# Four chained graph layers on one core: row sums divided out on GpSimd before the transposes, layer 0 multiplied by rows, query and key stacks copied without a spill

## What is computed

```python
# layer 0
agg = einsum('bij,bjf->bif', adj, x) / maximum(sum(adj, -1), 1e-6)
out = relu(concat([x, agg], 2) @ W.T)
# layer 1: e from x, alpha = adj * exp(leaky_relu(e)), T = alpha / (row sum + 1e-12)
out = relu(x @ Wk0 + (T @ x) @ Wk1 + (T @ T @ x) @ Wk2 + biases)
# layer 2: three times adj @ (x @ W) + b, the first two with relu
# layer 3: 8 heads of 32
scores = einsum('bhqd,bhkd->bhqk', q, k) * SCALE * (adj + adj)[:, None]
attn = softmax(scores, axis=-1)
ctx = einsum('bhqk,bhkd->bhqd', attn, v)
out = ctx @ Wo.T + bo
```

## Time and profile before

| | us |
|---|---|
| median of 3 runs (3450.55 to 3451.14) | 3451.12 |
| profiled execution, its own time | 3450.14 |
| its span | 3448.3 |
| PE busy | 3168.9 (92%) |
| DVE busy | 2149.7 (62%) |
| ACT busy | 1749.3 (51%) |
| POOL busy | 405.7 (12%) |

### The profile page before, as it was taken

How to read it: one execution, slowest core, us unless ns; L and a number is a source line. 1 busy time by engine, 2 the same in 40 slices (tenths; PEclk the granted TensorE clock), 3 DMA queues, 4 the chain that set the end, 5 groups by cost and what they waited for, 6 DMA issues and landing times.

```text
span 3448.3 us, 79514 instructions
## 1 busy us (share of the span) xinstructions
PE 3168.9 (92%) x27032; PEld 2727.9 (79%) x27032; DVE 2149.7 (62%) x3916; ACT 1749.3 (51%) x3025; POOL 405.7 (12%) x1613
## 2 busy tenths in 40 slices
PE   6999989999899998999989999899997999989998
PEld 5887779877798677986779877798776987779877
DVE  4636866268662685637856378553786537865387
ACT  3425844258442684426844268432674326743277
POOL 0101110011100111000110001100111001110011
PEclk9999999999999999999999999899998999989999
DMA  5113132131320313303133031330313303123120
GB/s 198 50 54 85 48 124 64 41 84 48 124 79 29 84 45 124 97 14 88 42 121 99 13 87 47 116 99 13 87 48 114 99 25 78 57 103 98 36 49 17
DMA packets 147694, 252.43 MB, mean 73 GB/s; under 512 B 11047, under 2 KB 112172, under 8 KB 147244
## 3 DMA queue, kind: packets, MB, share of 16 engines
q1 hardware_dynamic: 147244, 246.73, 22.2%
HBM read 146.03 MB, written 100.66 MB: 72 GB/s over the span
## 4 chain that ended last, share of the span: by engine, by line
PE 45%; issue 40%; DMA 5%; DVE 4%; POOL 3%; ACT 2%; DVEq 1%; SPq 0%; POOLq 0%; ACTq 0%
PE ps L655 10%; PE ps L645 7%; PE ps L454 7%; PE ps L456 7%; PE ps L455 7%; PE ps L668 5%; DMA qk_spill<-u_lo 3%; DMA k_stack<-qk_spill 2%; PE ps L683 1%; POOL shift L427 1%; POOL vare L420 1%; DVE r L1307 1%; DVE stats L1104 1%; DVE xr L1338 1%; POOL rstd L423 0%
## 5 line engine op out<-in xcount | busy, mean ns | idle before, releaser
L1307 DVE CUSTOM_DVE_ANT_0 r<-ps,adjn 128x1024 f32<-128x1024 f32 x512 | 621.9, 1217 | 31.5 <-PE ps L655 19.5
L1014 ACT ACTIVATE r<-r,nmax 128x1024 f32<-128x1024 f32 x512 | 585.7, 1144 | 80.7 <-POOL nmax L446 80.7
L655 PEld LDWEIGHTS ps<-ident,r 128*128 128x128 f32 x4096 | 471.0, 142 | 118.6 <-DVE pt L1316 75.6
L655 PE MATMUL ps<-ident,r 128*128 128x128 f32 x4096 | 551.3, 278 | 3.5 <-DVE pt L1316 3.5
L454 PE MATMUL ps<-u_hi,t_hi 128*128 128x256 f32 x1536 | 447.0, 291 | 4.1 <-DVE u_lo L1067 4.1
L455 PE MATMUL ps<-u_lo,t_hi 128*128 128x256 f32 x1536 | 439.0, 286 | 0.0
L456 PE MATMUL ps<-u_hi,t_lo 128*128 128x256 f32 x1536 | 438.8, 286 | 0.0
L1316 DVE COPY pt<-ps 128x512 f32<-128x512 f32 x512 | 353.1, 690 | 136.3 <-PE ps L655 136.2
L645 PE MATMUL ps<-k_stack,q_stack 96*128 96x512 f32 x1024 | 377.9, 452 | 54.5 <-DVE mmax L1307 32.4
L816 ACT ACTIVATE pt<-ps 128x512 f32<-128x512 f32 x512 | 304.9, 595 | 180.1 <-PE ps L655 175.4
L454 PE MATMUL ps<-w_hi,xt_hi 128*128 128x256 f32 x1024 | 302.0, 295 | 32.3 <-DVE xt_lo L1074 27.1
(11 more groups left out here) (172 smaller groups left out, 5556.1 us busy)
## 6 DMA issues: line engine op xcount, KB each, us to landing
adjn<-in_adj SPq DMA_DIRECT2D x64, 512.0 KB, 3.4
t_spill<-t_hi SPq DMA_DIRECT2D x64, 512.0 KB, 2.6
t_spill<-t_lo SPq DMA_DIRECT2D x64, 512.0 KB, 3.7
t_hi<-t_spill SPq DMA_DIRECT2D x32, 1024.0 KB, 5.4
t_lo<-t_spill SPq DMA_DIRECT2D x32, 1024.0 KB, 8.0
q_stack<-qk_spill SPq DMA_DIRECT2D x24, 512.0 KB, 6.9
k_stack<-qk_spill SPq DMA_DIRECT2D x24, 512.0 KB, 7.6
xn<-in_x SPq DMA_DIRECT2D x16, 512.0 KB, 4.0
```

Of the source, the lines that this page charges most:

```text
L655: last = pe.transpose(ps[:, TP + half, t * P:(t + 1) * P], r[:, u % RSLOTS, (TPH * half + t) * P:(TPH * half + t + 1) * P], ident)
L1014: act.activation(r[:, s % RSLOTS, :], r[:, s % RSLOTS, :], ACT.Exp, bias=nmax[:, s % 4:s % 4 + 1], accum_out=prow[:, qt % 2, h:h + 1]).the ...
L1307: dve.tensor_tensor_reduce(out=r[:, s % RSLOTS, :], in0=ps[:, 2 * (s % 2):2 * (s % 2) + 2, :].rearrange("p a c -> p (a c)"), in1=adjn[:, q ...
```

## The change

In layer 3 every unit has its own place for the row sum (`prow`, four slots). GpSimd raises it to the power -1 and multiplies the 128 x 1024 exponentials by it (a `tensor_scalar` in place) before TensorE transposes them: `transpose_p` waits for `p_scaled`. The inversion on VectorE, `denominators`, `spread_denominators`, their copies and `c_f` are gone; `c_hi` and `c_lo` come from bank 6 directly. Both transposes and output change banks: the halves rotate over banks 4, 5 and 7, and the output goes to the second half of bank 6. `LAG` is 4, `r` has a fifth slot (`r_last`, in the area of `u_lo`), and of head 7 ScalarE copies both halves. The values are projected within steps 0 to 3 of the loop. Heads 4 to 7 of the stacks are copied from `u_hi`, `u_lo` straight into `q_stack`, `k_stack`, in 24 DMAs of 32 partitions, with a semaphore for each head; VectorE waits for all of them in step 4, ahead of its first write to `r_last`, and ScalarE in step 4, ahead of its first write to `pt`.

In layer 0 all of `adj` and x are transposed first, through banks 4, 5, 2 and 3, with `g` = x times the aggregate's weights between; then `row_product` multiplies `adj` by `g` row block by row block, 24 matmuls of 256 columns each, and VectorE applies the inverse degree as it adds. VectorE's row sums follow its last subtraction.

```diff
...
-    LAG = 3
+    LAG = 4
...
-    TP_L0 = sum([halves_of("adj", j) for j in range(NT)], []) + x_units(0, 0) + x_units(0, 1)
+    adj_units = lambda *js: sum([halves_of("adj", j) for j in js], [])
+    TP_L0 = adj_units(0, 1) + x_units(0, 0) + adj_units(2, 3) + x_units(0, 1) + adj_units(4, 5, 6, 7)
...
+        if n < len(TP_L0):
+            return ((4, 5, 2, 3)[n % 4],)
...
-    PR_ORDER = ([("layer 0", t) for t in range(NT)] +
+    PR_ORDER = ([("g", k) for k in range(PAIRS)] + [("layer 0", t) for t in range(NT)] +
...
-        PSLOTS, RSLOTS = 6, 4
+        PSLOTS, RSLOTS = 6, 5
...
+        r_of = lambda u: r_last[:, :] if u % RSLOTS == RSLOTS - 1 else r[:, u % RSLOTS, :]
...
+        on_act = lambda u, half: half == 1 or u % H == H - 1
...
+        def p_bank(u, half):
+
+            return ps[:, (4, 5, 7)[(2 * u + half) % 3], :]
...
-                for n in range(2):
-                    sp.wait_ge(pr_free, nth(b, PR_UNITS, pr["qk", (1, n, 1)] + 1))
-                    at = slice(n * N, (n + 1) * N)
-                    sp.dma_start(qk_d[n, 0], f32(u_hi[:, at])).then_inc(qk_out[n], 16)
-                    sp.dma_start(qk_d[n, 1], f32(u_lo[:, at])).then_inc(qk_out[n], 16)
-                    sp.wait_ge(qk_out[n], nth(b, 32, 32))
-                    hi, lo = (qk_d[n, k].rearrange("(g p) n -> p g n", p=HD) for k in range(2))
-                    stack = q_stack if n == 0 else k_stack
-                    for part, src in enumerate((hi, hi, lo) if n == 0 else (lo, hi, hi)):
-                        sp.dma_start(f32(stack[HD * part:HD * (part + 1), G:2 * G, :]),
-                                     src).then_inc(stacked[n], 16)
+                for g in range(G):
+                    rows = slice(HD * g, HD * (g + 1))
+                    for n in range(2):
+                        if g == 0:
+                            sp.wait_ge(pr_free, nth(b, PR_UNITS, pr["qk", (1, n, 1)] + 1))
+                        at = slice(n * N, (n + 1) * N)
+                        hi, lo = f32(u_hi[rows, at]), f32(u_lo[rows, at])
+                        stack = q_stack if n == 0 else k_stack
+                        for part, src in enumerate((hi, hi, lo) if n == 0 else (lo, hi, hi)):
+                            sp.dma_start(f32(stack[HD * part:HD * (part + 1), G + g, :]), src).then_inc(stacked[g], 16)
+                for g in range(G):
+                    sp.wait_ge(stacked[g], nth(b, 16 * 6, 16 * 6))
...
+                    if 1 <= u <= UNITS:
+                        k = (u - 1) % 4
+                        pool.wait_ge(exp_done, nth(b, UNITS, u))
+                        pool.tensor_tensor(rprow[:, k:k + 1], prow[:, k:k + 1], inverse[:, :],
+                                           ALU.pow).then_inc(inv_ready, 1)
+                        pool.wait_ge(inv_ready, nth(b, UNITS, u))
+                        pool.sem_inc(passed_pool, 1)
+                        pool.tensor_scalar(r_of(u - 1), r_of(u - 1), rprow[:, k:k + 1], 0.0, ALU.mult,
+                                           ALU.add).then_inc(p_scaled, 1)
...
-                pe.wait_ge(exp_done, nth(b, UNITS, u + 1))
+                pe.wait_ge(p_scaled, nth(b, UNITS, u + 1))
+                if u == 1:
+                    pe.wait_ge(pr_free, nth(b, PR_UNITS, PR_UNITS))
                 for half in range(HALVES):
-                    if u >= 1:
-                        pe.wait_ge(p_dve if half == 0 else p_act, nth(b, UNITS, u))
+                    n = 2 * u + half
+                    if n >= 3:
+                        pe.wait_ge(*p_moved(b, *divmod(n - 3, 2)))
                     for t in range(TPH):
-                        last = pe.transpose(ps[:, TP + half, t * P:(t + 1) * P],
-                                            r[:, u % RSLOTS, (TPH * half + t) * P:(TPH * half + t + 1) * P], ident)
+                        last = pe.transpose(p_bank(u, half)[:, t * P:(t + 1) * P],
+                                            r_of(u)[:, (TPH * half + t) * P:(TPH * half + t + 1) * P], ident)
                     last.then_inc(p_full, 1)
 
...
-                    pe.wait_ge(c_raw, nth(b, NT, qt))
+                    pe.wait_ge(c_ready, nth(b, NT, qt))
+                if g == 1 and qt >= 1 and part == 0:
+                    pe.wait_ge(h_sum, nth(b, NT, qt))
...
-            def denominators(b, qt):
-                pe.wait_ge(rp_ready, nth(b, NT, qt + 1))
+            def output(b, qt):
+                pe.wait_ge(c_ready, nth(b, NT, qt + 1))
                 if qt >= 1:
                     pe.wait_ge(h_sum, nth(b, NT, qt))
-                pe.matmul(ps[0:H, 7, 0:P], rprow[:, qt % 2, :], ident[:, :], start=True, stop=True).then_inc(rt_full, 1)
-
...
-                for j in range(NT):
-                    if j + 1 < NT:
-                        transpose_adj(b, 0, j + 1)
-                    pe.wait_ge(tp_free, nth(b, TP_UNITS, tp_a(0, j) + 2))
-                    if j % TPH == 0:
-                        pe.wait_ge(x_split, nth(b, 2, j // TPH + 1))
-                    transposed_products(j)
-                transpose_x(b, 0)
+                transpose_adj(b, 0, 1)
+                transpose_x_half(b, 0, 0)
+                transpose_adj(b, 0, 2)
+                transpose_adj(b, 0, 3)
                 pe.wait_ge(drained, b + 1)
+                project_pairs(b, "g", W_L0G, xt_wait(b, 0), range(2))
+                transpose_x_half(b, 0, 1)
+                transpose_adj(b, 0, 4)
+                transpose_adj(b, 0, 5)
+                project_pairs(b, "g", W_L0G, xt_wait(b, 0), range(2, PAIRS))
+                transpose_adj(b, 0, 6)
+                transpose_adj(b, 0, 7)
+                self_part = lambda t: project(pr_bank(b, pr["layer 0", t])[:, 0:F], W_L0X, t).then_inc(pr_full, 1)
+                self_part(0)
+                self_part(1)
                 for t in range(NT):
-                    if t == 0:
-                        pe.wait_ge(tp_free, nth(b, TP_UNITS, tp_x(0, 1) + 2))
-                    if t == NT - 1:
+                    row_product(b, t, AF_L0)
+                    if t + 2 < NT:
+                        self_part(t + 2)
+                    if t == NT - 3:
                         transpose_x_half(b, 1, 0)
-                    dst = pr_bank(b, pr["layer 0", t])
-                    project(dst[:, 0:F], W_L0X, t)
-                    if t % TPH == 0:
-                        pe.wait_ge(u_ready, nth(b, 4 + PAIRS, 2 * (t // TPH) + 2))
-                    project(dst[:, F:2 * F], W_L0G, t, gh, gl).then_inc(pr_full, 1)
 
 
...
-                project_pairs(b, "values", W_V, xt_wait(b, 3))
-                pe.wait_ge(pr_free, nth(b, PR_UNITS, PR_UNITS))
+                pe.wait_ge(pr_free, nth(b, PR_UNITS, pr["qk", QK[-1]] + 1))
                 for n in range(COPIES):
                     stack_copies(b, n)
                 scores(b, 0)
-                for s in range(UNITS + 10):
+                for s in range(UNITS + 11):
                     if s + 1 < UNITS:
                         scores(b, s + 1)
+                    if s < PAIRS:
...
-                    if s >= 11 and (s - 11) % H == 0 and (s - 11) // H < NT:
-                        denominators(b, (s - 11) // H)
-                    if s >= 13 and (s - 13) % H == 0 and (s - 13) // H < NT:
-                        spread_denominators(b, (s - 13) // H)
...
+                        for half in range(HALVES):
+                            if on_act(u, half):
+                                act.wait_ge(p_full, nth(b, 2 * UNITS, 2 * u + half + 1))
+                                copy(pt[:, u % PSLOTS, TPH * half:TPH * (half + 1), :].rearrange("p t q -> p (t q)"),
+                                     p_bank(u, half)).then_inc(p_act, 1)
...
+                        if s >= 4:
+                            act.wait_ge(inv_ready, nth(b, UNITS, s - 3))
+                        act.activation(r_of(s), r_of(s), ACT.Exp, bias=nmax[:, s % 4:s % 4 + 1],
+                                       accum_out=prow[:, s % 4:s % 4 + 1]).then_inc(exp_done, 1)
...
+                        act.wait_ge(ctx_done, nth(b, 2 * NT, 2 * qt + 2))
...
+                        copy(c_hi[:, :, :].rearrange("p g q -> p (g q)"), ps[:, 6, 0:2 * P]).then_inc(c_hi_ready, 1)
...
+                dve.wait_ge(deg_ready, nth(b, 2, 1))
+                for t in range(NT):
+                    dve.wait_ge(pr_act, nth(b, NT + NT // 2, t + 1))
+                    dve.sem_inc(pr_free, 1)
+                    dve.wait_ge(acc_full, nth(b, AF_PER, AF_L0 + t + 1))
+                    dve.scalar_tensor_tensor(out=ev[:, t % 2, F:2 * F], in0=ps[:, ACC + t % 4, 0:F],
+                                             scalar=rdeg[:, t:t + 1], in1=ev[:, t % 2, 0:F], op0=ALU.mult,
+                                             op1=ALU.add).then_inc(acc_free, 1)
+                    dve.wait_ge(acc_free, nth(b, 3 * NT, t + 1))
+                    relu_residual(b, 0, t)
+                    tile_stats(b, 0, t)
...
```

(22 more changed lines are left out.)

258 lines of the change are left out of this document (97 added, 161 removed).

## The result

The changed kernel takes **3345.7 us** (median of 4 runs, 3344.8 to 3346.7) against 3451.1 (4 runs, 3450.6 to 3451.5): a ratio of 0.9695, 95% interval 0.9678 to 0.9711, or 105 us less. The forecast was 137 us less, so the sign was right, and about three quarters of the forecast gain came. The profiled execution took 3344.8 us, its span is 3343.0; that of the kernel before was 3448.3.

What follows compares the result with a forecast made beforehand. TensorE, busy 92% of the span, was taken to bound the kernel. Gains of 11.6 us in layer 3 and 5.5 in layer 0, times 8 elements, made 137 us off 3450.14: 3314 us, range 3235 to 3475.

Steps and rivals of the forecast that it cites:

- TensorE's own work in the block, 16.3 us: Layer 3's loop: TensorE's work for 8 units and six output matmuls, 16.3 us a block once the denominators go.
- TensorE's waits, 1.3 us a block: Layer 3's loop: TensorE's waits for VectorE plus a remainder, 1.3 us, making the block 17.6 us.
- The hand layout: Layer 3's block of 8 units laid out by hand with three banks: TensorE waits about 0.4 and 0.7 us.
- The whole loop: Layer 3's 54 units up to unit 63's scores: forecast gain 4.1 us an element.
- The block of GpSimd, 8.0 + 8x = 16.3: Layer 3: GpSimd's work a block, x being one unit's scaling, taken as 1.04 us, with 2.34 the other end.
- Rival 1: Layer 3: GpSimd becomes the bound and the kernel slower, scaling over 1.46 us; 3590 us at 1.72; chance 0.17.
- Rival 2: Layer 3: GpSimd becomes the bound a little, 18 to 19.5 us a block, 3340 to 3450 us; chance 0.10.
- Rival 4: Waits for VectorE take up all that leaves TensorE (block 18.2), layer 0 gains 2.5; 3371 us; chance 0.08.
- Entry: Into layer 3's loop: values move into steps 0 to 3; first scores gain 5.05 us, unit 9's 1.6 more.
- rival 3: Copies into layer 3's stacks come late; 3450 us at half the rate, 3370 at three quarters; chance 0.07.
- Layer 0: Layer 0 takes 50.5 us against 56.0, a gain of 5.5 us an element; ends 2.5 and 7.5.
- The turn and the tail: After layer 3's last scores: tail 14.3 us against 15.1, gain 0.8; no change at the turn to the next element.

Runs made afterwards that it cites:

- xr_late: Kernel after, with VectorE's addition of the projected output to x put behind the step's mask and maximum instead of ahead of them; 3316.7 us.
- no_scale: Kernel after, with GpSimd's scaling pass over the exponentials left out, so the outputs lack the division by the row sums; 3330.5 us.
- quarter_more: Kernel after, with one more GpSimd pass of 256 columns in each unit, into a spare tile nobody reads; 3508.4 us.
- best: Kernel after with xr_late's edit, one more transposes copy a block on ScalarE, and the next x's second half loaded behind the output's stores; 3296.6 us.
- recip_dve: Kernel best with the reciprocal of the row sums made by VectorE in place of GpSimd's power; 3265.5 us, the fastest version.

## Why the prediction was right, and where it was not

- **TensorE's own work in the block, 16.3 us: right.** It was added up from the earlier trace rows. From start to start of the scores the block of the kernel after, with the place that xr_late freed, is 2.55 + 2.55 + 2.16 + 1.26 + 2.55 + 2.55 + 1.36 and a last 1.36 without its wait, 16.3 us. The fastest version, which still waits a little for masks, takes 16.93. (By busy time TensorE has 16.8 us a block and 1.4 idle; a matmul's modelled end covers the start of each wait, so this split gives less to the waits.)
- **TensorE's waits, 1.3 us a block: the term that failed.** This is the term of the sum that was too small: 18.17 - 16.3 = 1.9. By no_scale 1.7 of them come from VectorE and TensorE alone, 0.2 from GpSimd. The hand layout took the two waits behind the residual and at the block's end for 0.4 and 0.7 us, which are nearly the 0.54 and 0.71 of the trace, and added 0.2 as a remainder; but from start to start they are 0.79 and 0.94 (2.05 us from 747.92 to 749.97, where xr_late takes 1.26, and 2.30 from 756.42 to 758.72, where a unit without context takes 1.36). The first of them was counted but not priced as what it is, a wait that the change adds by moving the sum ahead of the mask: what is queued behind it on VectorE is a mask that TensorE needs at once. xr_late, which takes this one step back, is worth 0.57 us a block, as much as was missed, though it stops at GpSimd's chain. The whole loop cost 27 of the 31 us.
- **The block of GpSimd, 8.0 + 8x = 16.3: too small by 1.3.** x is 1.08 us from start to start, 1.12 busy, close to the 1.04 from the affine selects and far from 2.34: the choice between the ends was right. The rest is the power to its dependent, 0.77 where the row of the normalisation had 0.63 (0.21 us of idle time behind the busy 0.55). GpSimd was at 17.6, with 0.55 us a block to spare. The forecast also had `nmax` reach ScalarE while that still copied; instead ScalarE waits for it in 34 of 40 units, at little cost, since no_scale cut these waits from 13.7 to 3.9 us and gained 0.19 us a block. And GpSimd's share of the span is 36%, not near half. The two passes measured here stream a column in 0.93 ns. The Trainium skill (GPSIMD Engine Reference, Performance versus the Vector engine) puts a body of up to two operations at 1.03 cycles an element, at 1.2 GHz an estimate of 0.86 ns: the measured rate is 8% slower, close enough for the choice.
- **Rival 1 was nearer than its 0.17 seems.** It wanted x over 1.46; quarter_more, which stands for x at 1.5, took 3508 us, 57 over the kernel before. By the slope above, 0.3 us more in the scaling would have used up the whole gain.
- **Rival 2 came true in part.** It wanted 18 to 19.5 us a block from slower GpSimd steps or 0.1 us more in each wait; the time lies in its range, and 0.19 us of the block are GpSimd's. But no_scale, 15 us faster at most, shows that it wasn't the main cause. It became the bound in xr_late and in best.
- **Rival 4 came true by half.** Its block of 18.2 us, with waits for VectorE taking back what left TensorE, is what was measured (18.17). Its other half, a layer 0 that gains 2.5, was not: layer 0 gained 6.8. Its 3371 us missed by 25 us, the forecast's 3314 by 32, and the range of 3235 to 3475 holds both: that the time lies in it does not tell the two apart, the block does. Of the 4.1 us an element that the forecast gave the loop, 0.7 came.
- **Entry: right.** 6.7 us an element up to unit 9 against 6.65, and the stacks' DMAs were no wait: rival 3 had no part in it. The SP queue's row of one issue of the 24, of 0.6 us where I had 0.9:

```profile
699.08 0.59 SPq L362 DMA_DIRECT2D q_stack<-u_lo  x1
```

- **Layer 0: 6.8 for 5.5, the clock.** The forecast let five pairs of half banks run cold, 10 us. Stretches of the kernel after from the first transpose to layer 1:

```profile
452.07:455.53 3.46, 3.46 (x16) 3.46 (x17) 1.38 (x2) 1.79 (x3) 0.00 (x0) 0.50 0.06 12
455.53:456.80 1.27, 1.27 (x10) 1.27 (x10) 1.08 (x2) 0.84 (x2) 0.00 (x0) 0.69 0.45 181
456.80:458.95 2.15, 2.04 (x19) 1.63 (x17) 2.06 (x4) 2.15 (x5) 0.00 (x0) 1.00 1.01 400
458.95:471.23 12.28, 12.02 (x103) 11.60 (x102) 9.93 (x17) 8.67 (x17) 0.00 (x0) 1.00 1.02 402
471.23:500.92 29.69, 28.43 (x239) 28.23 (x238) 21.89 (x42) 6.92 (x15) 6.13 (x24) 1.00 0.21 83
```

and of the kernel before:

```profile
886.40:889.86 3.46, 2.10 (x9) 1.70 (x10) 0.88 (x2) 1.51 (x3) 0.00 (x0) 0.50 0.17 50
889.86:893.00 3.14, 3.14 (x11) 2.55 (x12) 3.00 (x4) 2.39 (x4) 0.00 (x0) 0.50 0.62 247
893.00:895.00 2.00, 2.00 (x7) 1.53 (x7) 2.00 (x3) 0.27 (x1) 0.00 (x0) 0.62 0.48 184
895.00:897.00 2.00, 2.00 (x15) 1.74 (x14) 1.22 (x2) 0.51 (x2) 0.00 (x0) 1.00 1.02 395
```

  The five pairs took 6.9 us. TensorE works without a gap from 452.07 and has the full clock (2.4 GHz) by 456.80; before it paused after its first transposes, was at half of it (1.2 GHz) up to 893 and at the full one by 895. The phase up to the row products took 19.2 us where 21.9 was forecast, that of the row products 29.7 for 28.6.
- **The turn and the tail: too small, or left out.** I counted the tail's 0.8 us and no change in what follows. But the turn runs from the issue of x, which follows the last context; a shorter output behind it gave nothing, and one more step of lag (12.6 us from the start of the last scores to the last context matmul, 11.2 before) is late by all of it. This cost 9 + 4 us. It is read from the traces: no run has the change with `LAG` 3, so neither this price nor the cover that `LAG` 4 gives the transposes was tested by itself. Layer 0's 11 us over the forecast made up for most of it, by luck.

## What to carry to other kernels

When work is taken from the engine that bounds a loop, look for what its busy time has covered on the others, by laying each partner's chain start to start through one period: here 1.05 us a block went and 0.95 came back, until a sum that waits 0.47 us in VectorE's order was put behind the mask and a column operation of GpSimd given to another engine. Judge an in-order engine by its period from start to start, not by its busy share: at 87% busy GpSimd was full to within 3%, and a quarter of a pass more made the whole change a loss. Reordering within an engine has to be checked for rings over the neighbours: the order that saved GpSimd its 0.21 us tied each exponential to the one before.

## What was not expected of the hardware

- A power of one column on GpSimd is 0.55 us busy, and what needs its result starts 0.21 us after its end; a reciprocal of one column on VectorE is 0.16 us. Moving it was worth 31 us (best to recip_dve).
- At the loop's turn the packet of instructions (16 KB, 1.0 us) went only when the bulk load ahead of it was through, and TensorE resumed 2.5 us after it began. A megabyte of load issued at that point cost 2.3 us a turn against a quarter of it.
- The granted clock of one unchanged stretch of 205 to 210 us differs by a hundredth or two from element to element of the same run, worth some 1.5 us each.
